# Attention in runs of four steps, row maxima by half units in three PSUM banks, and queries prepared by sequence, in a two-layer transformer block on one Trainium2 core

## What is computed

```
q = proj(q_vec, Wq, bq)            # q_vec: x normalised, H = 16, D = 16
k = proj(k_vec, Wk, bk)            # 4096 context rows
v = proj(v_vec, Wv, bv)
energy = einsum('bhqd,bhkd->bhqk', q, k) / sqrt(D)
energy = where(mask_input == 0, -1e9, energy)
attn = softmax(energy, axis=-1)
context = einsum('bhqk,bhkd->bhqd', attn, v)
return einsum('bse,fe->bsf', context, Wo) + bo
```

## Time and profile before

| | |
|---|---|
| time, median of 3 runs | 1009.53 us (1006.78 to 1012.37) |
| the profiled execution | 1008.83 us around a span of 1007.0 us |
| TensorE busy | 911.6 us (91% of the span) |
| VectorE, ScalarE, GpSimd busy | 604.2, 479.5, 105.7 us |
| granted TensorE clock, mean over the span | 0.96 of full |
| chain that ended last | TensorE 78%, VectorE 8%, ScalarE 6%, issue 3%, DMA 3% |

### The profile page before, as it was taken

One profiled execution on the slowest core, in us unless ns is written; L12 is line 12 of the kernel. 1 busy time (PEld: TensorE's weight loads), 2 busy tenths in 40 slices (PEclk: granted clock), 3 DMA queues, 4 the chain that ended last, 5 costly groups with the idle time before them and its releaser, 6 DMA issues.

```text
span 1007.0 us, 15376 instructions
## 1 busy us (share of the span) xinstructions
PE 911.6 (91%) x6060; PEld 541.9 (54%) x6060; DVE 604.2 (60%) x1073; ACT 479.5 (48%) x951; POOL 105.7 (11%) x118
## 2 busy tenths in 40 slices
PE   6778899999999999999988899498999989988788
PEld 2344444444555555555444677354875854555656
DVE  5658587777875448888823686847414127188240
ACT  2322466777775557777787433223413110676111
POOL 3311011111000000000000100101000007155000
PEclk9989999999999999999999899678999989999889
DMA  9663843543422122223332500716508250000000
GB/s 358 167 203 126 251 117 101 152 138 115 131 64 75 32 54 64 74 64 113 121 121 96 213 1 1 251 42 217 222 26 321 93 167 1 1 1 2 0 1 21
DMA packets 66372, 108.68 MB, mean 108 GB/s; under 512 B 6902, under 2 KB 40438, under 8 KB 64374
## 3 DMA queue, kind: packets, MB, share of 16 engines
q1 hardware_dynamic: 64092, 100.35, 31.7%
q10 hardware_dynamic: 2208, 7.34, 1.8%
HBM read 93.77 MB, written 13.89 MB: 107 GB/s over the span
## 4 chain that ended last, share of the span: by engine, by line
PE 78%; DVE 8%; ACT 6%; issue 3%; DMA 3%; SPq 1%; POOL 0%; ACTq 0%; DVEq 0%
PE psum L1759 13%; PE psum L1741 10%; PE psum L1712 9%; PE psum L2116 6%; PE psum L2087 5%; PE psum L1876 5%; PE psum L1696 4%; PE psum L2179 4%; PE psum L1686 4%; PE psum L1889 3%; ACT arena L734 3%; DVE arena L1071 2%; DMA arena<-wvT 2%; PE psum L2227 2%; PE psum L2315 1%
## 5 line engine op out<-in xcount | busy, mean ns | idle before, releaser
L1071 DVE TENSOR_REDUCE arena<-psum 128x1 f32<-128x1024 f32 x256 | 300.6, 1219 | 111.3 <-PE psum L1712 111.2
L734 ACT ACTIVATE arena<-psum 128x512 f32<-128x512 f32 x512 | 264.5, 605 | 62.1 <-PE psum L1741 61.0
L1712 PE MATMUL psum<-arena 96*128 96x512 bf16 x512 | 151.5, 381 | 20.1 <-DVE arena L1071 11.3
L1741 PE MATMUL psum<-arena 99*128 99x256 bf16 x1024 | 160.2, 274 | 8.9 <-ACT arena L734 4.8
L1741 PEld LDWEIGHTS psum<-arena 99*128 99x128 bf16 x1024 | 79.5, 97 | 107.0 <-ACT arena L734 50.2
L1759 PE MATMUL psum<-arena 128*32 128x256 f32 x2048 | 136.8, 385 | 0.0
L1759 PEld LDWEIGHTS psum<-arena 128*32 128x32 f32 x2048 | 53.5, 109 | 75.4 <-ACT arena L734 36.9
L1686 PE MATMUL psum<-arena 128*128 128x512 f32 x128 | 65.0, 637 | 8.8 <-DMA arena<-ctxT 5.5
L1712 PEld LDWEIGHTS psum<-arena 96*128 96x128 bf16 x512 | 48.7, 98 | 38.9 <-DVE arena L1071 20.1
L627 POOL TENSOR_TENSOR arena<-arena 128x512 bf16<-128x512 f32 x34 | 41.6, 1223 | 206.7 <-DVE arena L1057 196.0
L1696 PE MATMUL psum<-arena 128*128 128x256 f32 x256 | 62.1, 387 | 0.0
(11 more groups left out here) (241 smaller groups left out, 972.9 us busy)
## 6 DMA issues: line engine op xcount, KB each, us to landing
arena<-kparts SPq DMA_DIRECT2D x192, 128.0 KB, 3.0
kparts<-arena SPq DMA_DIRECT2D x32, 384.0 KB, 3.3
arena<-ctxT SPq DMA_DIRECT2D x18, 512.0 KB, 5.4
arena<-ctx SPq DMA_DIRECT2D x2, 4096.0 KB, 15.3
arena<-mask SPq DMA_DIRECT2D x8, 1024.0 KB, 5.2
arena<-mask ACTq DMA_DIRECT2D x4, 1024.0 KB, 10.5
arena<-ctxT SPq DMA_DIRECT2D x1, 4096.0 KB, 14.1
arena<-ctxT SPq DMA_DIRECT2D x4, 1024.0 KB, 8.2
```

The costliest lines, as they stand in the source:

```text
L734: nc.scalar.activation(PR[step % 4][:, pair * CH:(pair + 1) * CH], ring_bank(slot), ACT.Exp)\
L1071: nc.vector.tensor_reduce(MX[g % 2][:, col:col + 1], unit_banks(n).rearrange("p b n -> p (b n)"), AX.X, ALU.max).then_inc(s_maxed, 1)
L1712: last = nc.tensor.matmul(out, q, KST[g % 2][0:ROWS, j, at], start=True, stop=not masked, skip_group_check=True)
L1741: last = nc.tensor.matmul(ring_heads(slot)[:, u, :], KST[gg % 2][0:KROWS, j, kc * P:(kc + 1) * P], QST[0:KROWS, G * g + j, b * S:(b + 1) * S],
```

## The change

- **Runs.** The loop goes in runs of four steps (`RUN`): turned scores and units of four steps, then the four steps are weighed in the same run, with no lag. Key pieces stand between scores and weighing; all value pieces of sequence 1 lie in group 3, two per run.
- **Banks.** The ring has four banks (3 to 6). The units have three (0 to 2), and VectorE reduces each half unit of 512 columns by itself, with a semaphore per half: half h may be written when half h - 3 is reduced.
- **Start.** Queries are turned, projected, split, stored and loaded by sequence, those of sequence 0 between the first and second key chunk; the mask's conversion moves behind them; loads of three context chunks move from ScalarE's queue to SP's, and all mask loads come at once. Eleven rounds instead of twelve.
- **Second cross-attention.** Turning and weighing are interleaved by quarters of a block; `e_att` counts quarters.

```diff
-RING = 3
+RING = 4
 SLOTS = 6
-BRANCH = 3
-EARLY = 2
+BRANCH = 4
 PLACES = 6
 AHEAD = 6
 RAMP = 5
-VALUES_AT = {3: 0, 4: 1, 5: 2, 6: 3, 8: 4, 9: 5, 10: 6, 11: 7}
-ROUNDS = 12
-UNITS_AT = {4: (2, 2), 5: (3, 3), 6: (3, 3), 7: (2, 2), 8: (2, 2), 10: (3, 3), 11: (2, 0)}
+VALUES_AT = {3: 0, 4: 1, 5: 2, 6: 3, 7: 4, 8: 5, 9: 6, 10: 7}
+ROUNDS = 11
+RUN = 4
+RUNS = KC // RUN
+UNITS_AT = {4: (2, 2), 5: (3, 3), 6: (3, 3), 7: (3, 3), 8: (2, 2), 9: (3, 3)}
 
...
             return COLT[:, COL_AT[name] + i:COL_AT[name] + i + 1]
 
         def ring_bank(slot):
-            return psum[:, 4 + slot % RING, :]
+            return psum[:, 3 + slot % RING, :]
 
         def ring_heads(slot):
             return ring_bank(slot).rearrange("p (j n) -> p j n", j=2)
 
-        def unit_banks(n):
-            return psum[:, 2 * (n % 2):2 * (n % 2) + 2, :]
+        def half_bank(h):
+            return psum[:, h % 3, :]
 
...
             for gg in range(GROUPS):
-                for m in range(KC // 2):
-                    if m == KC // 2 - 1 and gg + 1 < GROUPS:
+                for m in range(RUNS):
+                    if gg and m == 0:
+                        copy_weighed(gg - 1)
+                    for step in steps_of(gg, m):
+                        exps(step)
+                    if m == RUNS - 1 and gg + 1 < GROUPS:
                         copy_tops(gg + 1)
-                    exps(KC * gg + 2 * m)
-                    exps(KC * gg + 2 * m + 1)
                     if keys_at(gg, m):
                         copy_keys(1, *keys_at(gg, m))
...
             def row_tops(n):
                 g, i = divmod(n, UNITS)
-                col = QUARTERS * (i % 8) + i // 8
-                dve.wait_ge(s_ready, n + 1)
-                nc.vector.tensor_reduce(MX[g % 2][:, col:col + 1], unit_banks(n).rearrange("p b n -> p (b n)"),
-                                        AX.X, ALU.max).then_inc(s_maxed, 1)
+                for half in range(2):
+                    col = 2 * QUARTERS * (i % 8) + 2 * (i // 8) + half
+                    dve.wait_ge(s_ready, 2 * n + half + 1)
+                    nc.vector.tensor_reduce(MX[g % 2][:, col:col + 1], half_bank(2 * n + half), AX.X, ALU.max)\
+                      .then_inc(s_maxed, 1)
 
             def split_max(g):
                 n = 5 * g
-                dve.wait_ge(s_maxed, UNITS * (g + 1))
-                nc.vector.tensor_reduce(M8, MX[g % 2].rearrange("p (m c) -> p m c", c=QUARTERS), AX.X, ALU.max)\
+                dve.wait_ge(s_maxed, 2 * UNITS * (g + 1))
+                nc.vector.tensor_reduce(M8, MX[g % 2].rearrange("p (m c) -> p m c", c=2 * QUARTERS), AX.X, ALU.max)\
                   .then_inc(m_step, 1)
...
-            for c in range(EARLY):
-                for i in range(2):
-                    split_keys(0, c, i)
-                if c == 0:
-                    copy_turned_x()
-            for i in range(8):
+            copy_turned_x(0)
+            split_keys(0, 0, 0)
+            split_keys(0, 0, 1)
+            split_queries(0)
+            copy_turned_x(1)
+            split_keys(0, 1, 0)
+            split_keys(0, 1, 1)
+            for i in range(4):
                 mask_part(i)
-            split_queries(0)
-            dve.wait_ge(mask_counted, 1)
-            nc.vector.tensor_reduce(FLAGF[0:1, 0:1], psum[0:1, 2, :], AX.X, ALU.min).then_inc(mask_step, 1)
+            split_queries(1)
+            split_keys(0, 2, 0)
+            split_keys(0, 2, 1)
+            for i in range(4, 8):
+                mask_part(i)
+            split_keys(0, 3, 0)
+            dve.wait_ge(first_psum, 3)
+            nc.vector.tensor_reduce(FLAGF[0:1, 0:1], psum[0:1, 1, :], AX.X, ALU.min).then_inc(mask_step, 1)
             dve.wait_ge(mask_step, 9)
             nc.vector.tensor_scalar(FLAG, FLAGF[0:1, 0:1], 0.0, None, ALU.is_lt).then_inc(mask_step, 1)
-            split_queries(1)
-            for c in range(EARLY, ROUNDS):
+            split_keys(0, 3, 1)
...
                 gg, k = divmod(step, KC)
                 if k == 5 and gg:
                     normalise(gg - 1)
-                if k % 2 == 1 and step >= 3:
-                    before = divmod(step // 2 - 1, KC // 2)
+                if k % RUN == 1 and step >= RUN:
+                    before = divmod(step // RUN - 1, RUNS)
                     if keys_at(*before):
                         split_keys(1, *keys_at(*before))
...
             def scores(n, masked):
                 g, i = divmod(n, UNITS)
                 quarter, j, qt, b = i // 8, i % 8 // 2, i % 2, g // GPB
-                if n >= 2:
-                    pe.wait_ge(s_maxed, n - 1)
+                if n % (GPB * UNITS) == 0:
+                    pe.wait_ge(q_stacked, 16 + 96 * (b + 1))
                 if i % 8 == 0:
                     pe.wait_ge(k_stacked[g % 2][quarter], 96 * (g // 2 + 1))
                 q = QST[0:ROWS, G * (g % GPB) + j, b * S + qt * P:b * S + (qt + 1) * P]
                 for half in range(2):
                     at = slice((2 * quarter + half) * CH, (2 * quarter + half + 1) * CH)
-                    out = unit_banks(n)[:, half, :]
+                    h = 2 * n + half
+                    out = half_bank(h)
+                    if h >= 3:
+                        pe.wait_ge(s_maxed, h - 2)
                     last = nc.tensor.matmul(out, q, KST[g % 2][0:ROWS, j, at], start=True, stop=not masked,
                                             skip_group_check=True)
                     if masked:
                         last = nc.tensor.matmul(out, IDENTB, MASKB[:, qt, at], start=False, stop=True,
                                                 skip_group_check=True)
-                last.then_inc(s_ready, 1)
+                    last.then_inc(s_ready, 1)
 
             def turn_max(gg):
                 for pair in range(2):
...
                 turn_max(0)
                 for gg in range(GROUPS):
-                    for m in range(KC // 2):
-                        if m == KC // 2 - 1 and gg + 1 < GROUPS:
-                            turn_max(gg + 1)
-                        for step in (KC * gg + 2 * m, KC * gg + 2 * m + 1):
+                    for m in range(RUNS):
+                        for step in steps_of(gg, m):
                             turned_scores(step, masked)
                             for n in range(units_by(step - 1), units_by(step)):
                                 scores(n, masked)
+                        if m == RUNS - 1 and gg + 1 < GROUPS:
+                            turn_max(gg + 1)
                         if keys_at(gg, m):
                             project_keys(1, *keys_at(gg, m))
-                        if gg and m == 1:
+                        if gg and m == 0:
                             turn_context(gg - 1)
-                        if gg or m:
-                            weigh_values(KC * gg + 2 * m - 2)
-                            weigh_values(KC * gg + 2 * m - 1)
-                        if values_after(gg, m):
-                            project_values(1, *values_after(gg, m))
-                        if gg + 1 == GROUPS and m == KC // 4:
+                        for step in steps_of(gg, m):
+                            weigh_values(step)
+                        if gg == 3:
+                            project_values(1, m, 0)
+                            project_values(1, m, 1)
+                        if gg + 1 == GROUPS and m == RUNS // 2:
                             pe.wait_ge(on["w_summed"], 2)
-                            pe.wait_ge(s_maxed, GROUPS * UNITS)
+                            pe.wait_ge(s_maxed, 2 * GROUPS * UNITS)
                             nc.tensor.matmul(psum[:, 0, 0:2], ONES, WSUM, start=True, stop=True)\
                               .then_inc(on["w_total"], 1)
-                weigh_values(GROUPS * KC - 2)
-                weigh_values(GROUPS * KC - 1)
                 turn_context(GROUPS - 1)
...
-            for w in range(2, 4):
-                turn_exps(w)
-                weigh_context(w)
+            for n in range(4):
+                turn_exps(2, n)
+            weigh_context(2, 0)
+            turn_exps(2, 4)
+            turn_exps(2, 5)
+            weigh_context(2, 1)
+            turn_exps(2, 6)
+            turn_exps(2, 7)
+            weigh_context(2, 2)
```

369 lines of the change are left out of this document (216 added, 153 removed).

## The result

The changed kernel takes 1077.12 us (median of 4 runs, 1073.51 to 1079.56) against 1010.95 for the kernel before beside it: 1.0668 times, 95% interval 1.0638 to 1.0697. It is slower, as forecast, but by 66 us and not by 33; the time lies outside the range of 1023 to 1060.

What follows compares the result with a forecast made beforehand. The prediction took TensorE to bound the loop now, and VectorE's queue of half reductions to become critical in each run. 1008.8 + 46 (loop) - 6 (start) - 7 (second cross-attention) = 1042 us, range 1023 to 1060.

Steps and rivals of the forecast that it cites:

- The loop's walk: Attention loop: half reductions 0.60 us apart in three banks make a plain run 6.18 us against 5.70; loop +46 us.
- The minus 6 of the value group: Loop groups 3 and 4: four ScalarE banks end the waits for three ring banks, saving 6 us.
- rival 2: Loop: halves stand about 0.66 us apart, VectorE's chain carries 14 us more, 1056 us; chance 0.07.
- rival 4: Loop: waits let the granted clock fall, each 3.4 us at half speed costs 1.7, ten make 1059 us; chance 0.04.
- 1.07 per split, 2.9 per hand-over: Loop: VectorE's key splits cost 17.1 us over 16 runs; split_max and normalise at six hand-overs add 10 us.
- rival 1: The forecast itself: halves in three banks bind every loop run, 1042 us (1026 to 1056); chance 0.72.
- the start: Up to the loop: no wait for the queries' load, slower score rounds; net -6 us, between -12 and +3.
- walked through, the branch comes near 36: Start: VectorE's list up to the mask flag grows by one copy and some splits; branch near 36 us.
- one key and one value piece before the first unit: Start: two pieces of 1.72 us each follow the branch; first unit at 39.5, put at 41 with queueing.
- first unit to loop about 71: Score rounds ahead of the loop: about 71 us against 64.1, with near 3.5 of wait for the fourth key quarter.
- rival 3: Start: first unit no earlier, queries' stores and loads queue behind three context chunks; 1055 us; chance 0.07.
- The second cross-attention: Behind the loop: weighing quarters between turned groups cover the copies; -7 us, between 0 and -9.

Runs made afterwards that it cites:

- experiment 5: The changed kernel with 438 matmuls that write where nobody reads, placed ahead of TensorE's waits at 116 loop halves: 1057.01 us, 1.0475 times the kernel before.
- experiment 9: The changed kernel, runs of four kept, with halves in four banks, three for ScalarE, x loaded first, old table of rounds: 994.86 us, 0.9853 times the kernel before.
- Experiment 10: The changed kernel, eleven-round table kept, with halves in four banks, three for ScalarE, lagged runs of two, x loaded first: 996.19 us, 0.9876 times the kernel before.
- experiment 2: The kernel before with half units in three banks and four banks for ScalarE, still in lagged runs of two steps: 1029.28 us, ratio 1.0177.

## Why the prediction was wrong, step by step

**The loop's walk was right.** A plain run was put at 6.18 and takes 6.19, with waits of 0.08, 0.30 and 0.32 for the predicted 0.07, 0.33 and 0.33; a key run 8.97 for 9.0, a value run 9.73 for 9.6; the reductions stand 0.60 apart. With the clock held up (experiment 5) the loop is +49.6 us for the predicted +46, and it is not a sum of errors that cancel: groups 0 and 1 with their key pieces are +28.3 for a predicted 29, groups 3 and 4 +5.5 for 5, group 5 +5.3 for 5.5. One cause in it is only partly right. The minus 6 of the value group was put down to a fourth bank for ScalarE; experiment 9 has three, and groups 3 and 4 take 122.8 us in it against 127.1 before, so the new order of the value pieces gives most of it. The figure of the Trainium skill, Perfetto Trace Analysis, section Optimizing Scalar/DVE Operations, about 125 ns of overhead per instruction on PSUM, would have put the halves 0.66 apart; rival 2 is out.

**The first failed step is the clock, which the sum has at nothing.** The prediction priced a falling clock rightly (1.7 us for each 3.4 at half speed, +17 for ten), but only as rival 4 with a chance of 0.04, because a stretch with 82% busy still had 0.97. The mean busy share didn't decide it. The changed loop's mean is 90% (449.59 of 499.00), higher than that, and the clock fell all the same. The stretch from 54 to 118 was even stronger evidence than its 0.97 says, since the lower clock in it ends at 58:

```profile
58.00:118.00 60.00, 48.73 (x198) 29.69 (x196) 42.95 (x49) 19.18 (x31) 8.07 (x7) 1.00 0.54 162
```

TensorE waits there nine times for VectorE, 8.6 us in all and 1.2 at most, at the full clock. So the evidence was real, and it did not carry over. What the changed loop has besides is VectorE's key split, normalise and split_max in one place, so that TensorE waits up to 2.4 us at a time and, in most key runs, 1.2 us. The prediction had these very waits (1.07 per split, 2.9 per hand-over) in its sum and didn't ask what the clock makes of them. Experiment 5 shows the clock as the cause of 16 us in the loop and nearly 5 behind it. So the case that came is rival 1 with rival 4 on top, which the range ought to have held. Which of the waits let the clock fall stays open.

The Trainium skill, TensorE: Matmul & The Clock Gate, section What's actually happening, says that a block of the hardware sets TensorE's clock by how busy the engine has been of late. Experiment 5 agrees: only what TensorE does in the waits was changed, and 16 us of the loop went.

**The second is the start, -6 for +7.3.** Three terms of it:
- "walked through, the branch comes near 36": 47.76. 5.6 us of this are the moved first loads: the diff puts x behind the column constants and asks for four masks at once, and x landed at 13.64 instead of 8.62; the prediction didn't price moved loads at all. The other part is the list: up to the branch it is 8 us longer than before (25.9 against 18.1), where a branch near 36 leaves 2 (TensorE's first piece behind the branch starts at 33.91 in the kernel before). Three more key splits stand in it, of which some casts take 1.26 instead of 0.43, and one more query split of 2.4.
- "one key and one value piece before the first unit": 3.44, right.
- "first unit to loop about 71": 74.1, with the wait for the fourth key quarter at 3.80 for 3.5, and a stretch at the half clock that begins in this very wait (104.6 to 111.4). Experiment 10 shows both without the three banks.

So rival 3 came in effect (first unit only 2.8 us earlier than before), by another mechanism than queues behind the context chunks.

**The second cross-attention was about right** (5.0 us once the clock's share is taken out, for -7; that the kernel with it alone is 6.8 faster is in part luck with the clock). In the changed kernel only 2.4 us are left, because the 142 us between the loop and it take 3 us longer: the clock of the first 25 us behind the loop is 0.73 for 0.86. Only part of the 3 us is TensorE's own work (busy 123.7 us against 122.6), the rest are longer waits; with the loop's waits filled (experiment 5) this stretch takes 140.0 us.

```profile
624.30:649.30 25.00, 21.30 (x101) 15.20 (x94) 11.31 (x37) 6.93 (x14) 5.57 (x20) 0.73 0.62 233
```

## What to carry to other kernels

A bank less for a producer and consumer in lockstep costs little where other work lies between and the consumer has nothing else to do (0.17 us per four steps), and much where scores come in a row (0.53 against the same run with four banks, experiment 9) or where the consumer's queue holds other work (nearly 12 us over the 16 key pieces of experiment 2, the clock's share taken out): walk the longest row, not the mean. When such a walk finds waits on TensorE that were not there, add the clock to the sum: here 34 waits for VectorE, 33 us together, came with another 16 us in the loop and nearly 5 behind it. And if loads change places at the start, price the landing time of the one that everything hangs on.
